# Row scatters of a fused four-layer kernel: one block behind the attention loop instead of between its last steps

## The reference, cut to what matters

```python
xn = _layernorm(x)
# s: attention with 16 heads of 64, causal mask to 0 before softmax, residual and second layernorm
q, k, v = heads(layernorm(xn))
s = resid_mid + layernorm(resid_mid)          # resid_mid = xn + attention output
# g: 16 experts, two per token
probs = softmax(xn @ Wr + br);  topk_w, topk_idx = top_k(probs, 2)
h = gelu(layernorm(xn @ W1[e] + b1[e]));  out = h @ W2[e] + b2[e]
g = silu(sum over the token's two experts of topk_w * out)
x = x + s * g
```

## Time and profile before

| What | Value |
|---|---|
| Median of 3 runs | 1665.83 us (1661.51 to 1669.95) |
| The profiled execution's own time | 1672.02 us |
| Its span, first to last instruction | 1670.1 us |
| Mean granted clock of TensorE in it | 0.874 |
| Instructions | 21792 |
| Attention loop of layer 0, first to last product by GpSimd | from 76 to 562 us |
| First load of sorted rows | 566 us |
| First gather at the end of layer 0 | 669 us |

### The profile page before, as it was taken

How to read it: one execution, slowest core, us unless ns; L and a number is a source line. 1 busy time by engine, 2 the same in 40 slices (tenths; PEclk the granted TensorE clock), 3 DMA queues, 4 the chain that set the end, 5 groups by cost and what they waited for, 6 DMA issues and landing times. The chain is left out here.

```text
span 1670.1 us, 21792 instructions
## 1 busy us (share of the span) xinstructions
PE 1285.4 (77%) x7188; PEld 869.9 (52%) x7188; DVE 1070.8 (64%) x2574; ACT 724.9 (43%) x1526; POOL 600.8 (36%) x597
## 2 busy tenths in 40 slices
PE   1799999998987777376677985785784886788885
PEld 0355554654644555254564663553563465566664
DVE  1366676778686343455655995996897699724334
ACT  1345555455443234123236653662672573343332
POOL 1243444343338422422311442343243144225551
PEclk9998999999988678677778897797897799799998
DMA  7200000000000112430000000000000000001113
GB/s 176 71 1 1 1 1 2 1 1 1 1 4 29 51 51 70 129 111 13 13 1 1 1 1 0 1 1 0 1 1 1 1 1 1 26 12 34 35 33 89
DMA packets 54315, 40.36 MB, mean 24 GB/s; under 512 B 13175, under 2 KB 46685, under 8 KB 54205
## 3 DMA queue, kind: packets, MB, share of 16 engines
q1 hardware_dynamic: 35516, 23.91, 4.9%
q0 software_dynamic: 4544, 9.32, 2.0%
q10 hardware_dynamic: 14146, 5.75, 1.6%
HBM read 25.92 MB, written 13.04 MB: 23 GB/s over the span
## 5 line engine op out<-in xcount | busy, mean ns | idle before, releaser
L753 POOL TENSOR_TENSOR PR<-PR,R 128x256 f32<-128x256 f32 (+3 forms) x128 | 161.5, 1262 | 280.8 <-DVE R L1205 276.3
L1617 POOL TENSOR_TENSOR SA<-SA,H 128x512 f32<-128x512 f32 x64 | 81.8, 1277 | 258.2 <-DVE H L1844 258.2
L1839 DVE TENSOR_TENSOR_SCAN H<-DAS,H 128x512 f32<-128x512 f32 x128 | 174.6, 1402 | 0.0
L1022 ACT ACTIVATE PR<-banks,NM 128x129 f32<-128x129 f32 (+3 forms) x256 | 132.6, 527 | 47.5 <-DVE NM L1182 45.0
L415 PE MATMUL banks<-BCR,identR 96*128 96x512 f32 x256 | 110.7, 519 | 54.5 <-DVE H L1844 45.6
L415 PEld LDWEIGHTS banks<-we,HH 128*128 128x128 f32 x1024 | 145.3, 211 | 10.4
L415 PE MATMUL banks<-we,HH 128*128 128x128 f32 x1024 | 144.5, 294 | 0.0
L415 PEld LDWEIGHTS banks<-PTS,V 128*64 128x64 f32 x1280 | 72.9, 143 | 103.4 <-issue 97.1
L415 PE MATMUL banks<-XNT,we 128*128 128x512 f32 x256 | 120.7, 594 | 0.0
L415 PE MATMUL banks<-PTS,V 128*64 128x128 f32 x1280 | 105.0, 295 | 19.6 <-DVE PTS L1190 12.6
L1190 DVE COPY PTS<-banks 128x128 f32<-128x128 f32 (+3 forms) x128 | 62.2, 486 | 86.8 <-PE banks L893 83.8
(11 more groups left out here) (512 smaller groups left out, 2700.2 us busy)
## 6 DMA issues: line engine op xcount, KB each, us to landing
xsort<-zrow SPq DMA_DIRECT2D x1, 3072.0 KB, 13.1
XS<-xsort SPq DMA_DIRECT2D x12, 256.0 KB, 2.9
ysort<-PTS SPq DMA_DIRECT2D x12, 256.0 KB, 2.2
pj_stage<-in_L_ffn_w_proj SPq DMA_DIRECT2D x1, 2048.0 KB, 10.2
we<-in_L_ffn_we SPq DMA_DIRECT2D x1, 2048.0 KB, 9.3
we<-yrows SPq DMA_DIRECT2D x8, 256.0 KB, 4.9
X<-in_L_attn_resid_pre ACTq DMA_DIRECT2D x4, 256.0 KB, 4.7
xrows<-XN SPq DMA_DIRECT2D x4, 256.0 KB, 2.3
```

The costliest lines, as they stand in the source:

```text
L753: nc.gpsimd.tensor_tensor(p, p, R[:, n, :].unsqueeze(2).to_broadcast([P, 2, w]), ALU.mult).then_inc(pn, 1)
L1022: nc.scalar.activation(PR0[:, q % 2, s, OFF[t]:OFF[t] + w], ps2(n)[:, s, 0:w], ACT.Exp, bias=NM[:, n, s:s + 1], accum_out=L[:, n, s:s + 1] ...
L1617: nc.gpsimd.tensor_tensor(Y[m], Y[m], H[:, n % 2, m, :], ALU.add).then_inc(ya, 1)
L1839: nc.vector.tensor_tensor_scan(H[:, n % 2, m, :], DA[:, n % 4, m, :], H[:, n % 2, m, :], 0.0, ALU.mult, ALU.add).then_inc(scn, 1)
```

## The change

The 32 scatters are no longer issued in pairs behind the last sample's steps 16 to 31. They are issued one after the other in a loop of their own, behind the last step of the attention loop and ahead of the first inverse deviation of the feed-forward tiles, on the same queue and in the same order.

```diff
--- before.py
+++ after.py
@@ -784,9 +784,8 @@
                                 out_scale(b - 1)
                             if b and i == 17:
                                 out_norm(b - 1)
-                            if b == B - 1 and i >= 16:
-                                scatter(2 * (i - 16))
-                                scatter(2 * (i - 16) + 1)
+                        for i in range(2 * NT):
+                            scatter(i)
 
                         def unit_norm(u):
                             g.wait_ge(vr, u + 1)
```

## The result

The kernel after takes 1694.61 us in the median of 4 runs (1693.51 to 1695.62). The kernel before took 1664.1 (4 runs, 1661.51 to 1669.95). The ratio is 1.0178, 95% interval 1.0148 to 1.0208. The forecast was 1685, 1.1% slower.

The account below looks back on a forecast made before the run. GpSimd was taken to set the pace in the last half sample, TensorE elsewhere. The loop gives back 19.0 us, the scatter block then delays the load by a net 18.8: 1665.8 + 18.8 = 1684.6, said as 1685 us; range 1676 to 1698.

Parts of the forecast that it names:

- Step 2: Behind the loop: 32 scatters in a row, about 1.26 us apart, send the first sorted-row load out 18.8 us later.
- Step 3: TensorE after the pause: its restart at the feed-forward tiles is slow already in the kernel before, so nothing is added.
- Step 1: Attention loop from step 113 on: without scatters it gives back 19.0 us, bounds 12.5 to 21.4.
- Its own sign of being wrong: Loop estimate counts as wrong if the pairs from step 116 on stay over 13 us.
- My analogue in sample 1: Steps 49 to 52, normalisation between, no scatters: 9.57 us, taken for steps 113 to 116; 6.1 us gained.
- (a): Last half sample: GpSimd is the bound, so the move is neutral and time stays at 1666; chance 0.05.
- (b): Block behind the loop: scatters much shorter with VectorE quiet, so faster, 1655 us at 0.30 us each; chance 0.03.
- (c): Block behind the loop: queued transfers drain one by one at 2.25 us, load 49.5 later, 1715 us; chance 0.04.
- (d): First 34 us of feed-forward tiles: TensorE stays at clock 0.50, 12.2 us more, 1697 us; chance 0.02.
- Its long end: Slow bounds of the loop terms: 13.15 us for each full pair, 12.12 for the last stretch, 12.5 us gained.

Follow-up runs that it names:

- no_scatters: Kernel after with all 32 scatters left out, the feed-forward tiles of layer 0 reading zero rows; 1651.36 us.
- the later normalisation: Kernel after with GpSimd's output normalisation of sample 2 moved from behind step 113 to behind the block of scatters; 1689.47 us, ratio 1.0100 to the kernel before.
- before_norm_later: Kernel before, scatters still in the loop, with the output normalisation of sample 2 moved behind the last scatter; 1666.74 us, ratio 0.9975.
- half_back: Kernel after with 16 scatters put back in the loop, one behind each of steps 112 to 127, the other 16 behind it; 1677.39 us, ratio 1.0045.
- the measurement by itself: Kernel after with 40 linked VectorE operations, then 16 rounds of ping-pong with TensorE, added beside the block of scatters; one run, 1703.21 us.

## Why the prediction came out as it did

The side and the mechanism were right: the block comes to stand alone in front of the feed-forward tiles, and the loop gives back less than it costs. The size was too small, 18.8 us for 24.5.

In absolute time the forecast was 10 us low, 1684.6 for 1694.5. Of these, 5.7 are the size of the effect, and 4.2 are the starting point: the three runs shown gave the kernel before 1665.8, fourteen on chip 2 gave 1670.0.

**Step 2 was right.** From the end of the last product to the load: forecast 41.5 us, measured 41.86 and 41.9. The second scatter came 1.53 us behind the first (forecast 1.31), all others 1.26, and the load left 2.25 us behind the last scatter's start. 32 in a row kept the pace that eight gathers had.

**Step 3 was right, as far as the traces show.** The four transposes took 1.11 us as before, and the traces of no_scatters and of the kernel after show no cost of the pause beyond its length. The 4 us by which the medians differ further stay open.

**Step 1 failed, by 5 to 6 us.** Its own sign of being wrong, a pair over 13 us, came true for the pair behind step 116. By the ends of the last product the loop gave 562.53 - 548.73 = 13.8 us, not 19.0; measured from step 113 it is 14.0 in the first pair of traces and 13.0 in the second. Start of product to start of product, in us:

| Stretch | Forecast | After, first trace | After, second | With the later normalisation |
|---|---|---|---|---|
| Step 113 to 116 | 9.6 | 9.80 | 10.75 | 7.40 |
| Step 116 to 120 | 11.5 | 14.95 | 15.35 | 12.21 |
| Step 120 to 124 | 11.5 | 12.21 | 12.23 | 12.23 |
| Step 124 to the last product's end | 10.0 | 10.76 | 10.77 | 10.77 |
| Sum | 42.6 | 47.7 | 49.1 | 42.6 |

Three stretches were longer than forecast, for two reasons. The smaller one: I took two products of V off the ordinary pair, as TensorE was 98% busy in it, and gave VectorE's chain 0.6 us for it. The pair measured 12.2 with TensorE busy only 10.05 us of it. Once the products are out, I take it that the chain of row maximum, exponentials and reciprocal sets the rest; no run shows it by itself. That is 0.7 us a pair, and another 0.8 in the last stretch, 10.76 for 10.0. The larger one: the normalisation holds step 114 until 505.91 in the new kernel as well. My analogue in sample 1 ends at step 52 and gave the stretch up to step 116 rightly. But I let the next pair start from there as if nothing had happened. The products of 114 to 116 are GpSimd's, TensorE waited for them (1.06 and 1.51 us), fell to its 1.2 GHz level (mean granted clock 0.57 from 508.3 to 516.3) and did that work slowly in the next pair, which came out 3.5 us over forecast. The forecast put the clock at nothing inside the loop. The run with the later normalisation takes this away and has 12.21, so 2.7 of the 3.5 us are of this kind. The rows of sample 1 could not have warned of it: the pair behind the same normalisation took 13.14 us there, at a clock of 1.00.

That run also brings the loop to 42.6 us, the forecast's own sum. This is two errors that cancel, as the table shows, and no proof of its terms.

**The rivals.** (a), the neutral move: the share of GpSimd's queue was real. It was a little less full than I had read it, though, as the waits of 2.21 and 1.56 us for VectorE show. before_norm_later shows that GpSimd sets the pace there, and half_back that the second 16 scatters cost 12 us in the loop. But they cost 20 behind it, since about 16 are free in the loop and none is behind it. (b), a much shorter scatter with VectorE quiet: 958 against 990 ns. (c), transfers one by one: no, the load left 2.25 us behind the last scatter's start. (d), a long slow restart: no. Over the 34 us from the load on, TensorE was busy for the same 24.39 us as before, at a granted clock of 0.70 in place of 0.75; stretch of the kernel after:

```profile
590.59:624.59 34.00, 24.39 (x123) 19.90 (x123) 7.84 (x37) 5.56 (x10) 3.43 (x6) 0.70 0.19 55
```

**The range** of 1676 to 1698 held the time with some luck. Its long end had 13.15 us for a pair, which the first of them broke with 14.95; the other terms stayed under their long ends, and the spread of single runs that had been added took up the low starting point.

## What to carry to other kernels

Work that is issued from a queue with idle time is free up to that idle time, and what goes beyond it costs time (here about 12 us for 14 scatters of 1.3); behind the loop, in front of the work that waits for it, every piece costs in full. So the question to ask is how much fits, and here 16 scatters did, one per step. When a bound is taken off one engine, look for what else had been holding the steps on that engine's queue, and let the next stretch start from the engines' real lag, not from the last start of a product.

## What the runs showed of the hardware that was not expected

Beside a block of indirect transfers issued one behind the other by GpSimd, hand-overs from TensorE to VectorE that have nothing to do with it came late: one addition started 20 us after its product, and in the measurement by itself four of 16 rounds took 4.1 to 5.6 us instead of 1.18, none of 16 without the scatters. VectorE's operations that waited for nothing but their own predecessor ran on at 0.31 us beside the same transfers. It is one trace with and one without, and the cause is open.

The second thing is the spread. The same kernel before gave a median of 1664.1 in the first measurement (4 runs) and 1670.0 to 1671.2 on chips 2, 7 and 6, with single runs spread over 7 to 9 us. An effect of 0.3% needs a dozen runs here (the 95% intervals of the two runs of 12 were 0.21 and 0.25% wide, those of the runs of 5 up to 0.49%), and one profiled execution is not the median.
